# Blocks of 512 tokens in place of batches, and attention outputs packed by DMA in place of transposes, in a two-layer diffusion transformer kernel

## The reference

```python
# layer 0: adaptive norm (six shifts/scales and three gates per batch from cond)
h = ln(x) * (1 + sc) + sh
q, k, v = windows_of_128(roll(h @ w_qkv + b_qkv, -64))
x = x + g * (roll(softmax(q @ k.T / 4) @ v, 64) @ w_so + b_so)              # attention 1
s = (ln(x) * (1 + sc) + sh) @ w_q @ k_ctx.T / 4                              # 154 context tokens
top_s, top_i = top_k(s, 16)
x = x + g * (softmax(top_s) @ v_ctx[top_i] @ w_co + b_co)                    # attention 2
a, b = split((ln(x) * (1 + sc) + sh) @ w_m1 + b_m1)                          # 256 -> 2 x 1024
x = x + g * ((silu(a) * b) @ w_m2 + b_m2)
# layer 1
x = x + softmax(q @ k.T / 4) @ v @ wo + bo + t_sa                            # attention 3, all 1024 keys
x = x + softmax(mask(q @ k_ctx.T / 4)) @ v_ctx @ wo + bo + t_ca              # attention 4, 154 keys
x = x + gelu(ln(x) @ w1 + b1) @ w2 + b2 + t_mlp                              # 256 -> 1024 -> 256
```

## Time and profile before

| | |
|---|---|
| median of 3 runs | 1892.52 us (1890.46 to 1895.93) |
| profiled execution, its own time | 1887.55 us |
| its span, first to last instruction | 1885.5 us |
| mean granted TensorE clock | 0.855 of full speed |
| TensorE busy (matmul) | 1363.7 us, 72% |
| VectorE (DVE) busy | 1006.8 us, 53% |
| ScalarE (ACT) busy | 781.9 us, 41% |
| GpSimd (POOL) busy | 306.9 us, 16% |
| DMA, all 16 engines | 103.65 MB in 115850 packets, 55 GB/s over the span |

### The profile page before, as it was taken

One profiled execution on the slowest core, in us unless ns is written; L12 is line 12 of the kernel. 1 busy time (PEld: TensorE's weight loads), 2 busy tenths in 40 slices (PEclk: granted clock), 3 DMA queues, 4 the chain that ended last, 5 costly groups with the idle time before them and its releaser, 6 DMA issues.

```text
span 1885.5 us, 22617 instructions
## 1 busy us (share of the span) xinstructions
PE 1363.7 (72%) x7052; PEld 687.0 (36%) x7052; DVE 1006.8 (53%) x2985; ACT 781.9 (41%) x1626; POOL 306.9 (16%) x518
## 2 busy tenths in 40 slices
PE   2746566554556677756579989999889977778988
PEld 1324344332334333433334324322422214334556
DVE  4434335465776554566576446777777705643120
ACT  0113234244554445434133544566556663444221
POOL 7010010324444322232310000100010000100110
PEclk9968778575556989978799999999999999888999
DMA  4496874203111011012900040261322021440000
GB/s 159 149 157 129 147 128 83 39 30 74 22 22 25 1 22 22 1 48 76 137 6 1 1 71 31 84 98 22 45 53 35 12 42 22 87 65 6 12 14 23
DMA packets 115850, 103.65 MB, mean 55 GB/s; under 512 B 25114, under 2 KB 95503, under 8 KB 115475
## 3 DMA queue, kind: packets, MB, share of 16 engines
q1 hardware_dynamic: 114844, 101.82, 28.7%
q10 hardware_dynamic: 887, 0.39, 0.1%
HBM read 69.95 MB, written 31.63 MB: 54 GB/s over the span
## 4 chain that ended last, share of the span: by engine, by line
PE 34%; DVE 11%; ACT 5%; issue 5%; DMA 2%; SPq 1%; POOL 1%; ACTq 0%; DVEq 0%; POOLq 0%
PE bank L811 7%; DVE part_max L1200 5%; PE ring L708 5%; PE bank L746 5%; PE ring L725 5%; ACT pr L1003 3%; PE bank L782 2%; PE ring L661 2%; PE ring L685 2%; DVE x_hat L1174 1%; PE ring L669 1%; PE bank L814 1%; PE bank L816 1%; DMA ks<-ctx_mask 1%; PE bank L752 1%
## 5 line engine op out<-in xcount | busy, mean ns | idle before, releaser
L1003 ACT ACTIVATE pr<-bank 128x512 f32<-128x512 f32 x656 | 370.6, 596 | 266.7 <-PE bank L782 193.9
L1200 DVE TENSOR_REDUCE part_max<-bank 128x1 f32<-128x512 f32 x512 | 324.0, 684 | 180.9 <-PE bank L746 180.0
L746 PE MATMUL bank<-ks,qs 96*128 96x512 bf16 x512 | 199.4, 397 | 45.5 <-DVE part_max L1200 27.3
L782 PE MATMUL bank<-qs,ks 100*128 100x512 bf16 x512 | 193.6, 384 | 11.2 <-ACT pr L1003 9.4
L811 PE MATMUL bank<-pr,vs 128*32 128x512 f32 x1024 | 137.8, 610 | 22.2 <-ACT pr L1003 15.0
L842 PE MATMUL bank<-ident,probs 128*128 128x128 f32 x256 | 58.8, 371 | 130.4 <-POOL probs L1339 130.3
L746 PEld LDWEIGHTS bank<-ks,qs 96*128 96x128 bf16 x512 | 50.3, 98 | 248.4 <-DVE part_max L1200 191.4
L1234 DVE MAX8 top<-bank 128x8 f32<-128x154 f32 x256 | 69.9, 315 | 131.0 <-PE bank L831 130.8
L1020 ACT ACTIVATE exp_all<-bank,neg 128x154 f32<-128x154 f32 x256 | 85.2, 387 | 110.4 <-POOL neg L1328 109.7
L708 PE MATMUL ring<-h_t,w_m 128*128 128x512 f32 x256 | 130.7, 638 | 0.0
L1273 POOL TENSOR_SCALAR var_eps<-mean_var 128x4 f32<-128x4 f32 x24 | 5.8, 240 | 733.8 <-DVE mean_var L1165 733.4
(11 more groups left out here) (153 smaller groups left out, 2237.7 us busy)
## 6 DMA issues: line engine op xcount, KB each, us to landing
qs<-q_dram SPq DMA_DIRECT2D x192, 128.0 KB
q_dram<-parts SPq DMA_DIRECT2D x32, 384.0 KB, 2.5
ks<-k_dram SPq DMA_DIRECT2D x96, 128.0 KB
v_dram<-v_out SPq DMA_DIRECT2D x32, 256.0 KB, 2.9
vs<-v_dram SPq DMA_DIRECT2D x16, 512.0 KB
k_dram<-parts SPq DMA_DIRECT2D x16, 384.0 KB, 2.6
w_m<-in_L_xcond_w_m SPq DMA_DIRECT2D x1, 2048.0 KB, 9.0
w_m<-in_L_xcond_w_m SPq DMA_DIRECT2D x2, 1024.0 KB, 6.6
```

The lines of the kernel that those rows point to most:

```text
L746: last = nc.tensor.matmul(bank[:, :], qs[0:PACK, h, t * P:(t + 1) * P], ks[0:PACK, h, kc * 512:(kc + 1) * 512], start=True, stop=True)
L782: last = nc.tensor.matmul(bank[:, :], ks[0:FULL, h, kt * P:(kt + 1) * P], qs[0:FULL, h, qc * 512:(qc + 1) * 512], start=True, stop=True)
L1003: nc.scalar.activation(m.pr[:, u % NPR, :], m.bank[2 + u % 2][:, :], ACT.Exp).then_inc(m.s_free, 1)
L1200: nc.vector.tensor_reduce(m.part_max[:, slot, i // 2, i % 2:i % 2 + 1], bank[:, :], axis=AX.X, op=ALU.max).then_inc(m.m_read, 1)
```

## The change

Tokens go through all stages in four blocks of 512 (`NB`, `BT`, `T`) instead of batches, and attention in 64 groups of one block and 4 heads. The list `GROUPS` gives their order: attention 1 and attention 2 block by block, then attention 3 and, from its seventh group on, attention 4 interleaved with it. There are 4 slots for queries, 6 for keys (attention 3 takes two of them for a group) and 3 for context keys. The due times are all new, one `token_slots` for each block and stage.

The columns of the q and k weights are permuted on the host (`by_rows`), so that a group's 64 rows of parts lie in order of (d, head). A group is loaded by 6 DMAs in place of 12: three for queries and three for keys, of 3, 2 and 1 blocks of 16 partitions, whose access patterns have that number as outermost dimension; for keys it is one part repeated. Context keys and values of attentions 2 and 4 go by the same step. Each group has its `max_rows`. Values of attentions 1 and 3 stay in SBUF (`m.v`): `v_store` and `load_v` go.

The output of a group is copied to `o_t` (one copy of 512 columns) and moved by four DMAs of 16 partitions into `on`, packed as `y_mm` wants it; a fifth DMA spreads the denominators over 64 partitions of `den`. For each half of the heads DVE takes the reciprocal of 128x512 denominators and GpSimd multiplies. `o_turn`, `o_norm`, `on_turn` and `on_copy` are gone. In the top-k attention the offsets of the steps are others, exp_left is taken in place, and `c_pv` runs once for a group with 512 columns. The fills of `qs` and `ks` are single operations for all slots or put in the plan's order. The biases' rows come in one DMA; `res_row` has 4 slots in place of 2.

```diff
-Q_PART = (0, 1, 0, 2, 1, 0)
-K_PART = (0, 0, 1, 0, 1, 2)
+PRODUCTS = ((0, 3, 0), (3, 2, 1), (5, 1, 2))
...
+GROUPS = [(1, k, g) for k in range(NB) for g in range(GB)] + [(2, k, g) for k in range(NB) for g in range(GB)]
+GROUPS += [(3, 0, g) for g in range(GB)] + [(3, 1, 0), (3, 1, 1)]
+GROUPS += [(4, 0, 0), (3, 1, 2), (4, 0, 1), (3, 1, 3), (4, 0, 2), (3, 2, 0), (4, 0, 3), (3, 2, 1)]
...
+def after_group(plan, ready, gi, end):
+    a, k, g = GROUPS[gi]
+    plan.at(end, ("o_copy", gi), ("o_move", gi))
+    if g % 2 == 1:
+        plan.at(end + 4, ("norm", a, k, g // 2))
+    for later in range(gi + 1, min(gi + NQ + 1, len(GROUPS))):
+        if max(later - NQ, KEY_BEFORE[later]) == gi:
+            plan.at(max(end + 0.1, ready[GROUPS[later][:2]]), ("load", later))
+
+
+def topk_group(plan, ready, gi, start, step):
+    for t in range(BT):
+        for hf in range(2):
+            t0 = start + (t * 2 + hf) * step
+            plan.at(t0 - 1.05 * step, ("c_score", gi, t, hf))
+            plan.at(t0, ("c_top", gi, t, hf), ("c_neg", gi, t, hf))
+            plan.at(t0 + 0.45 * step, ("c_exp_all", gi, t, hf))
+            plan.at(t0 + 1.0 * step, ("c_exp_left", gi, t, hf), ("c_diff", gi, t, hf))
+        t1 = start + (t + 1) * 2 * step
+        plan.at(t1 + 0.6 * step, ("c_turn", gi, t))
+        plan.at(t1 + 0.9 * step, ("c_copy", gi, t))
+    end = start + 8 * step
+    plan.at(end + 1.2 * step, ("c_pv", gi))
+    after_group(plan, ready, gi, end + 1.9 * step)
...
+PACE = {1: (7, 7, 7), 3: (34, 7, 27), 4: (8, 7, 8)}
+TOP_STEP = 3.0
...
-                plan.at(t0 - 1.2 * step, ("c_score", gi, t, hf))
-                plan.at(t0 + 0.2 * step, ("c_exp_all", gi, t, hf))
-                plan.at(t0 + 1.1 * step, ("c_exp_left", gi, t, hf), ("c_diff", gi, t, hf))
-            plan.at(t1 + 0.3 * step, ("c_turn", gi, t))
-            plan.at(t1 + 0.6 * step, ("c_copy", gi, t), ("c_pv", gi, t))
...
-            for r in range(len(Q_PART)):
-                sp.dma_start(m.qs[slot][r * D:(r + 1) * D, :, :], m.q_dram[at][Q_PART[r], r0:r0 + HG * D, :].rearrange("(h d) t -> d h t", d=D)
-                             ).then_inc(m.qk_in[slot], 16)
+            for block, n, part in PRODUCTS:
+                to = slice(block * D, (block + n) * D)
+                sp.dma_start(m.qs[to, slot, :, :], m.q_dram[at][k, mt, 0:n, rows, :].rearrange("s (d h) t -> s d (h t)", h=HG)
+                             ).then_inc(m.group_in[slot], 16)
...
+                sp.dma_start(dest, src.rearrange("s (d h) t -> s d (h t)", h=HG).to_broadcast([n, D, size])).then_inc(m.group_in[slot], 16)
...
+        elif kind == "o_move":
...
+            for h in range(HG):
+                sp.dma_start(m.on[r0 + h * D:r0 + (h + 1) * D, g.on_slot(at, k), c, :], m.o_t[h * HW:h * HW + D, gi % NO, :]
+                             ).then_inc(m.o_moved[gi % NO], 16)
+            sp.dma_start(m.den[r0:r0 + HG * D, c, :], m.o_t[D:P:HW, gi % NO, :].unsqueeze(1).to_broadcast([HG, D, T])
+                         ).then_inc(m.o_moved[gi % NO], 16)
...
+        elif kind == "norm":
+            _, at, k, c = step
+            for group in (2 * c, 2 * c + 1):
+                gi = GROUP_AT[at, k, group]
+                dve.wait_ge(m.o_moved[gi % NO], O_MOVES * (gi // NO + 1))
+            nc.vector.reciprocal(m.den[:, c, :], m.den[:, c, :]).then_inc(m.recip_done, 1)
...
+        elif kind == "norm":
+            _, at, k, c = step
+            pool.wait_ge(m.recip_done, plan.order[step] + 1)
+            heads = m.on[:, g.on_slot(at, k), c, :]
+            nc.gpsimd.tensor_tensor(heads, heads, m.den[:, c, :], ALU.mult).then_inc(m.norm_done, 1)
...
+def by_rows(weight, first, n):
+
+    heads = weight[..., first:first + n].reshape(weight.shape[:-1] + (n // (HG * D), HG, D))
+    weight[..., first:first + n] = heads.swapaxes(-1, -2).reshape(weight.shape[:-1] + (n,))
```

More of the change, by code:

```diff
@@ L64 @@
+KEY_SLOT, KEY_BEFORE = key_slots()
+WEIGHED = [gi for gi in range(len(GROUPS)) if attention(gi) != 2]
+MAX_TURN = {gi: sum(1 for k in range(gi) if attention(k) != 2 and k % NQ == gi % NQ) for gi in WEIGHED}
 class Plan:
@@ L70, in at @@
     def at(self, time, *steps):
-        self.timed.append((time, len(self.timed), steps))
+        for late in range(2):
+            some = [step for step in steps if (step[0] in RING or step[0] == "down_part") == bool(late)]
+            self.timed.append((time, len(self.timed), some))
     def spread(self, slots, start, end):
@@ L90, in n, with place, projection_slots, mlp_slots @@
         return self.order[step]
[L93 to L110, removed]
+RING = ("y_mm", "hat_turn", "qk", "v", "ua", "ub", "ug", "down", "ck", "cv", "ctx_turn", "mcol", "mgate", "mbv", "mtp")
+def place(out, i, *steps):
+    while len(out) <= i:
+        out.append([])
+    out[i] += steps
+def projection_slots(s, k):
+    out = []
+    i = 0
+    for j, u in enumerate(Q_UNITS[s]):
+        place(out, i, ("qk", s, k, u))
+        place(out, i + 1, ("hi", s, k, u))
+        place(out, i + 2, ("split", s, k, u), ("qk_store", s, k, u))
+        i += 1
+        if s in HAS_V:
+            place(out, i, ("v", s, k, j))
+            place(out, i + 1, ("v_copy", s, k, j))
+            i += 1
     return out
-def mlp_slots(s, b, n):
+def mlp_slots(s, k):
     out = []
@@ new lines, in make_plan @@
+    for (s, k), (start, end) in stages.items():
+        plan.spread(token_slots(s, k), start, end)
+    ready = {}
+    for a, s in PROJECTION_OF.items():
+        for k in range(NB):
+            ready[a, k] = stages[s, k // 2 * 2 + 1 if a == 3 else k][1] + 1
+    plan.at(0, ("mcol", 0), ("mcol_add", 0))
+    plan.at(9, ("scale_wa",))
+    for i, time in enumerate((-1, 2, 22, 23)):
+        plan.at(time, ("fill", i))
+    mod = [[("mcol", 1)]]
+    for i in range(3):
+        mod += [[("mgate", i)], [("mgate_add", i), ("mbv", i)], [("mres", i), ("mtp", i)]]
+        mod[-3] += [("mtp_add", i - 1)] if i else [("mcol_add", 1)]
@@ L284, in make_plan @@
+    for gi in range(NQ):
+        plan.at(15 + 5 * (gi // 2), ("load", gi))
+    for gi, (a, k, g) in enumerate(GROUPS):
+        if a == 2:
+            topk_group(plan, ready, gi, starts[gi], TOP_STEP)
+        else:
+            weighed_group(plan, ready, gi, starts[gi], *PACE[a])
     plan.finish()
@@ L656, in tensor_program @@
                     pe.wait_ge(m.out_gated, plan.n("gate_out", j) + 1)
[L657 removed]
+                pe.wait_ge(m.norm_done, max(plan.n("norm", at, k, c) for c in range(CK)) + 1)
             since(pe, g.ring_turn(*step))
             for tt in range(2):
[L660 to L662 removed]
+                t = 2 * p + tt
```

1332 lines of the change are left out of this document (615 added, 717 removed).

## The result

The changed kernel takes 2208.38 us (median of 4, 2202.97 to 2212.72) where the kernel before takes 1894.22: ratio 1.1655, interval 1.1614 to 1.1696. It is 314 us slower. The prediction said 1647 us and faster; the slower rival, merged loads confined to a few engines, gave 2084.

The account below looks back on a forecast made before the run. No engine bounds the whole: DMA engines limit attention 1, VectorE's top-k loop attention 2, TensorE attention 3. 1887.6 + 11 − 160 − 97 = 1641.6, and 5 to the median: 1647 us; own range 1570 to 1740, whole range 1450 to 1800.

Parts of the forecast that it names:

- +11: Start and attention 1: earlier first matmul but slower group loads, ending at 345 us instead of 334.2.
- −160: Attention 2: top-k step falls from 2.92 us to 2.5 in the first 32 steps; 419 us against 579.
- −97: From attention 3 on: 100 us less from removed transposes and a moved block, less 3 us of longer waits.
- 19.4 GB/s an engine: Merged group loads: assumed rate of each confined DMA engine, from 310/16; 13.6 us a group.
- 218 us of loads: Attention 1: sixteen groups' merged loads at 13.6 us each.
- then the loads decide: Attention 1: loads, denominators' broadcast and other traffic, together 296 us, set its length, above PE and DVE.
- 168 us of a queue that mostly waits: nothing: SP queue: some 390 more DMAs at 0.43 us cost nothing unless a move stands behind a load's wait.
- hidden: Attention 3: a group's fullest engine carries 396 KB, 20 us, within the 28 or more the group lasts.
- my own split of the 248 ns: Reciprocal on DVE: two thirds of the 16-element operation's 248 ns would be paid at any size; 3.2 us taken.
- net I take 3: From attention 3 on: longer waits for stage input and `norm` on DVE, less interleaving's gain, cost 3 us.
- PE at 0.87 busy: From attention 3 on: assumed busy share, between 80 and 91%, turning 87 us of removed work into 100 us.
- Rival 3: Slower: confined loads at 9.6 GB/s an engine lengthen attention 1 by 217 us and later attentions by 220; 2084 us, chance 0.13.

Follow-up runs that it names:

- e9_bfills: The kernel before with GpSimd's fills put behind the fourth rstd instead of ahead of the first; 1905 us, ratio 1.006.
- e1_split: The changed kernel with each merged load of 48 or 32 partitions made as three or two DMAs of 16 partitions; 2071 us.
- e11_bmerge: The kernel before with 8 KB rows and the change's merged loads, six a group in place of twelve; 2080 us, ratio 1.098.
- e10_bwide: The kernel before with q and k columns permuted so that its twelve loads have rows of 8 KB instead of 2 KB; 1891 us, ratio 0.999.
- e13_btopk: The kernel before with the top-k loop's turn, copy and value step later, probs_t in two slots, exp_left in place; 1787 us, ratio 0.943.
- e6_late: e4_split_topk with later due times for `norm` and for each stage behind an attention; 2009 us.
- e4_split_topk: The changed kernel with split loads and the old top-k offset of exp_left and diff; 2057 us.
- e5_free: e4_split_topk with DVE's reciprocals on a spare tile, not waiting for denominators; division left out, output not the reference's; 1967 us.
- e14_apart_free: e12_apart with DVE's reciprocals on a spare tile without any wait; division left out, output not the reference's; 1930 us.
- e12_apart: e6_late with all groups of attention 3 first, then attention 4 block by block, not interleaved; 1984 us.

## Why the prediction was wrong

The three parts of the sum were +11 up to the end of attention 1, −160 for attention 2 and −97 from attention 3 on. Measured in the profiles they are +78, +1 and +237: misses of 67, 161 and 334 us. The confinement of the merged loads, which I had assumed, was right. What failed is what I put at nothing: the wait of everything that stands behind such a load, SP's issues, and DVE's in-order wait.

*Start.* The first m matmul came at 69.8 us, not 55; e9_bfills shows that the fills alone are worth 15 of the 40 us gained, and nothing at the end. I priced the fills ahead of the first rstd and not those behind it. Four x_hat instructions of DVE took 11.5 us on the chain that ended last, where e9_bfills has 1.4; the first of them took 10.5 and ended with a memset of GpSimd that ran beside it. The same comes again at 43.9 us:

```profile
11.51 11.47 DVE L1147 TENSOR_SCALAR x_hat<-x_sb,mean_var,rstd 128x256 f32<-128x256 f32 x4 [0.24 <-POOL rstd L1251]
11.53 10.33 POOL L1242 MEMSET ks<- 4x12288 bf16 x1
```

Together they cost 20 us, more than the 15 by which the start missed, and in e1_split both lie on the chain. That the memset holds DVE is my reading of the times; no run moved it.

*Attention 1.* It took 342 us, where the sum had 290 (from 55 to 345). The assumption that a copy is cut along its outermost dimension was right (DMA shares of 0.19 and 0.13 in e11_bmerge, 0.18 in the changed kernel). The Trainium skill's rule on copies outermost (page "DMA: Bandwidth & Descriptors", section "Rules for kernel authors") is borne out by both traces. The rate of 19.4 GB/s an engine was not too high: 22 to 26 were measured. That it was near is luck, since I took it for the length of the rows, which e10_bwide shows to do nothing. A group's last keys landed 11.3 to 11.8 us after their issue, against 13.6 in the sum. So the 218 us of loads hold, at some 180 (an estimate, 16 x 11.3); the failed step is "then the loads decide", that they run one behind the other with the stores fitted in between for a sixteenth of their bytes. The DMA share of 0.29 shows that they do not. The chain goes from a store that lands 11.4 us after its issue, behind loads, to ACT's copy, to the moves, to the next loads. With split loads the attention is still 285 us, and SP's issues are 40% of its chain: "168 us of a queue that mostly waits: nothing" was the other term at nothing.

*"Hidden" in attention 3.* The load of 396 KB was sized right (17.4 us from issue to landing of its last keys where the chain shows it, forecast 20), "hidden" was wrong: it delays what is sent behind it. The denominators landed 17.5 us after their issue, where e1_split has 7.7. In all, with the 57 us of attention 1, splitting the loads is worth 138 us.

*Top-k, −160.* Nothing came. The forecast said that the later turn and value step would free TensorE; on the kernel before they do, for 106 us (e13_btopk). In the changed kernel the gain was lost to the order of exp_left and neg (21 us), to `norm` standing in DVE's way at the start of each group (attention 2 is 44 us shorter in e6_late than in e4_split_topk), and, as far as the profiles show without a run for it, to 38 us more of DVE work. I saw the new offset of exp_left and did not ask which of two steps with the same due time is sorted first.

*Outputs by DMA.* The reciprocal was sized right (3.35 us for 3.2), partly by luck: my own split of the 248 ns gives 2.8. The failed step is "net I take 3": DVE's in-order wait costs 67 to 90 us by e5_free. Forecast were 8 us at a change of stage; but a `norm` is due 4 units behind every second group, the way takes 10 us, and DVE's reductions for the next group stand behind it.

*From attention 3 on, −97.* This is the largest miss, 334 us. The PE work did go: busy times clock is 832 x 0.83 = 690 us, against 567 x 0.97 + 132 x 0.85 and 130 x 0.99 in the last 143 us, 791, before. But PE at 0.87 busy was an assumption from stretches with few waits, and did not hold with twice as many groups: it was 832 of 1210 us, 0.69. Of the 237 us more, e1_split takes back 73. With the top-k order, the later `norm`, the attentions apart and DVE freed (e14_apart_free) 106 are left over the kernel before; the gains of the single runs do not simply add (e5_free had 59 on its own, 44 on top of e12_apart). These 106 us may lie with the finer blocks or with SP's queue; they are not settled singly.

Rival 3 had the sign and the confinement, but not the rate: its 9.6 GB/s an engine were 22 to 26. Its 2084 came nearer than my 1647 because a price too high for the loads stood in for the waits behind them, which it, too, counted as nothing, and it kept the −160 for the top-k loop. I gave it 0.13.

## What to carry to other kernels

Fewer DMAs are no gain if the merged pattern puts a count of 2 or 3 outermost: the same bytes took 189 us more. Price a slow DMA by what stands behind it on the queue and on its engines, not by its own bytes. A step that waits for a way through copy, queue and landing must be due later than that way takes, or the in-order engine hands the wait on to all. And in a loop over several in-order engines move the turn behind its producer before restructuring anything: later due times and a second buffer gave 5.7% on the kernel before.

## What the runs showed of the hardware

Loads whose outermost count is 3, 2 and 1 ran on three and then two of the sixteen DMA engines, at 22 to 26 GB/s each (DMA share 0.19 at 67 GB/s, 0.13 at 53). A store issued behind them landed after 11.4 to 11.9 us in place of a median of 2.5. Such a load is dearer to issue as well: the median on SP was 628 ns, against 420 for a load of 16 partitions in e10_bwide, and one took 20.9 us (one line's issues in e11_bmerge, ns min/median/max):

```profile
L1485 SPq DMA_DIRECT2D qs<-q_dram x96: 417/628/20945, 95.4 to 1877.4; - x96
```

The mean of the norm's product x_hat rose from 547 to 724 ns on DVE, but not its median (410 before, 408 after): single instructions took up to 10.5 us, those beside GpSimd's memset of 10.3 us.

```profile
L1147 DVE TENSOR_SCALAR x_hat<-x_sb,mean_var,rstd x96: 395/408/10506, 11.5 to 2161.8; 128x256 f32<-128x256 f32 x96
```

The reciprocal took 3352 ns for 512 columns, 2639 for 400 and 248 for 16: some 6.3 ns a column and 0.15 us beside (an estimate from the three).

Rows of 8 KB in place of 2 KB changed no time at 16 partitions (0.999).
